# Max pass in pairs of two through four PSUM banks, and two experts' lower products from 16-bit halves, in a one-core block kernel

## What is computed

```python
xn = layernorm(x)
# branch 1: state scan
xf = depthwise_conv3(xn) + conv_b
dt = sigmoid(xf @ dt_w.T + dt_b) * 0.099 + 0.001
s[t] = exp(dt[t] * A) * s[t-1] + dt[t] * xf[t] * b      # 16 states a channel
y[t] = sum(c * s[t])
# branch 2: attention, then all 8 experts, weighed by a gate
h = layernorm(xn) * g + b
q, k, v = h @ Wq, h @ Wk, h @ Wv          # 16 heads of 64
p = softmax(causal(10 * l2norm(q) * q_scale @ (l2norm(k) * k_scale).T))
o = layernorm(concat(p @ v) @ Wo)
gate = softmax(o @ gate_w + gate_b)
hid = gelu(einsum('bsd,edf->bsef', o, w1) + b1)          # 8 experts, 512 wide
moe = sum_e gate_e * (hid_e @ w2_e + b2_e)
out = x + y + layernorm(moe)
```

## Time and profile before

| | |
|---|---|
| Three executions | 1120.18, 1122.25, 1125.5 us |
| The profiled execution | 1120.17 us, of which the traced span is 1118.4 us |
| TensorE busy | 1075.0 us, 96% of the span |
| DVE busy | 959.6 us, 86% |
| ACT busy | 778.9 us, 70% |
| POOL busy | 277.7 us, 25% |
| TensorE's granted clock | 0.986 of full speed over the span |
| Chain that ended last | 89% of it on TensorE |

### The profile page before, as it was taken

How to read it: one execution, slowest core, us unless ns; L and a number is a source line. 1 busy time by engine, 2 the same in 40 slices (tenths; PEclk the granted TensorE clock), 3 DMA queues, 4 the chain that set the end, 5 groups by cost and what they waited for, 6 DMA issues and landing times.

```text
span 1118.4 us, 27576 instructions
## 1 busy us (share of the span) xinstructions
PE 1075.0 (96%) x10435; PEld 912.2 (82%) x10435; DVE 959.6 (86%) x2543; ACT 778.9 (70%) x1772; POOL 277.7 (25%) x328
## 2 busy tenths in 40 slices
PE   4877999999999999999999999999999999999997
PEld 1664888888888888888888888888888888888897
DVE  8988798898988989898898989889898888988763
ACT  5873948668595876859677594867759587685653
POOL 2340314224031231404123140412403132140200
PEclk9995999999999999999999999999999999999999
DMA  7010000000000000000000000000000000000000
GB/s 210 7 39 10 2 11 7 1 16 1 11 7 11 6 2 16 1 11 6 6 11 2 11 7 11 6 1 16 2 11 6 11 7 6 6 6 1 7 2 10
DMA packets 18722, 14.60 MB, mean 13 GB/s; under 512 B 2408, under 2 KB 16160, under 8 KB 18592
## 3 DMA queue, kind: packets, MB, share of 16 engines
q1 hardware_dynamic: 17680, 12.76, 3.8%
q10 hardware_dynamic: 912, 0.09, 0.1%
HBM read 10.75 MB, written 2.10 MB: 11 GB/s over the span
## 4 chain that ended last, share of the span: by engine, by line
PE 89%; DVE 4%; issue 3%; ACT 2%; POOL 1%; SPq 0%; DMA 0%; POOLq 0%; DVEq 0%; ACTq 0%
PE O L565 19%; PE O L468 14%; PE S L484 5%; PE U L547 5%; PE U L548 5%; PE U L549 5%; PE J L382 5%; PE S L449 4%; PE J L343 4%; PE U L449 4%; PE S L404 4%; PE J L344 3%; PE J L345 3%; PE S L400 3%; PE O L475 2%
## 5 line engine op out<-in xcount | busy, mean ns | idle before, releaser
L777 ACT ACTIVATE hid<-U,b1c 128x256 f32<-128x256 f32 x512 | 200.5, 474 | 174.8 <-PE U L549 174.7
L565 PE MATMUL O<-w2s,hid 128*128 128x128 f32 x2048 | 251.1, 276 | 0.0
L565 PEld LDWEIGHTS O<-w2s,hid 128*128 128x128 f32 x2048 | 238.6, 192 | 2.9
L928 POOL TENSOR_SCALAR_AFFINE_SELECT P<-P 128x512 f32<-128x512 f32 x128 | 85.0, 664 | 618.6 <-ACT P L750 618.5
L468 PEld LDWEIGHTS O<-Vx,P 128*128 128x128 f32 x1536 | 188.0, 192 | 30.2 <-issue 14.3
L468 PE MATMUL O<-Vx,P 128*128 128x66 f32 x1536 | 188.6, 273 | 3.6 <-POOL P L928 2.0
L1198 DVE TENSOR_TENSOR_SCAN st<-aexp,u 128x256 f32<-128x256 f32 x256 | 178.8, 698 | 0.4 <-issue 0.3
L920 POOL TENSOR_TENSOR raw<-raw,nr 128x512 f32<-128x512 f32 x124 | 132.8, 1097 | 134.9 <-DVE nr L1066 134.9
L1208 DVE SCALAR_TENSOR_TENSOR y<-st,bc,y 128x256 f32<-128x256 f32 x240 | 133.5, 556 | 8.5
L547 PE MATMUL U<-h2h,w1h 128*128 128x256 f16 x480 | 130.9, 273 | 0.0
L549 PE MATMUL U<-h2h,w1l 128*128 128x256 f16 x480 | 130.9, 273 | 0.0
(11 more groups left out here) (204 smaller groups left out, 2048.0 us busy)
## 6 DMA issues: line engine op xcount, KB each, us to landing
xin<-in_L_attn_x SPq DMA_DIRECT2D x16, 128.0 KB, 2.1
xres<-in_L_attn_x SPq DMA_DIRECT2D x16, 128.0 KB, 2.3
hid<-in_L_ffn_w SPq DMA_DIRECT2D x2, 1024.0 KB, 6.5
out_dram<-fin SPq DMA_DIRECT2D x16, 128.0 KB, 1.8
raw<-in_L_ffn_Wq SPq DMA_DIRECT2D x1, 512.0 KB, 4.7
raw<-in_L_ffn_Wk SPq DMA_DIRECT2D x1, 512.0 KB, 6.4
raw<-in_L_ffn_Wv SPq DMA_DIRECT2D x1, 512.0 KB, 7.4
wos<-in_L_ffn_Wo SPq DMA_DIRECT2D x1, 512.0 KB, 11.4
```

Of the source, the lines that this page charges most:

```text
L565: last = mm(O[e % 2][:, t * P:(t + 1) * P], hid[:, e % 2, m, t * P:(t + 1) * P], w2s[:, e * FC + m, :], start=(m == 0), stop=(m == FC - 1))
L777: fn(hid[:, e % 2, f % FC, :], U[q % 2][:, m * SEQ:(m + 1) * SEQ], ACT.Gelu_apprx_tanh, bias=b1c[:, f:f + 1], scale=1.0 / WS).then_inc(gel ...
```

## The change

The change has two parts, with moves that they need.

1. *Lower products of experts 0 and 1 from 16-bit halves* (`NH = 2`). Once, `w2` of the two experts is split into `w2h` and `w2l` (ACT in body 0, DVE in body 1). For each sequence ACT copies the 128x1024 hidden values to 16 bit (`hidden_high`), DVE takes the rest (`hidden_low`), and `expert_down` runs three 16-bit products where one float32 product stood: 24 instructions an expert for 16. `hidh` and `hidl` are one buffer each, so `hidden_high` of expert 1 waits for the lower product of expert 0. DVE also makes `gate64`, the two experts' gates divided by 64.
2. *Max pass two pairs at a time.* The two `J` banks, now one tile `J2`, serve beside `S2`. The products of two pairs stand one behind the other, then their masks. The pass has four turns, in m = 2, 5, 6 and 7.
3. *Moves.* `step_sizes(i+1)` and `turn(i+2)` go from m = 7 and 6 to m = 1 and into `S2`; `g_step` 6 goes to k = 8 of the attention half and `g_step` 7 to 9 to m = 1; the convolution goes to k = 9; one state leaves the attention half; the first turned maxima use a bank of `U2`. `turn_qk` 4 and 5 wait for the maxima of the first turn.

```diff
-        MAX_AT = {1 + p: (p,) for p in range(NP)}
+        MAX_AT = {2: 0, 5: 2, 6: 4, 7: 6}
...
+                if s > 0 and n in (4, 5):
+                    pe.wait_ge(mx_done, s * 2 * NP + 4)
...
+                elif p == 0:
+                    pe.wait_ge(ex_done, s * NP)
+                    pe.wait_ge(wo_copied, s)
+                    pe.wait_ge(tanh_done, s + 1)
+                    if s < LAST:
+                        pe.wait_ge(g_vec, (s + 1) * KG + 12)
+                    pe.wait_ge(t_lo, s * NL + 4)
+                    max_products(s, p)
+                else:
+                    pe.wait_ge(t_lo, s * NL + NL)
+                    pe.wait_ge(mx_done, s * 2 * NP + 2 * p)
+                    max_products(s, p)
+                max_products(s, p + 1)
+                max_masks(s, p)
+                max_masks(s, p + 1)
...
-                pe.wait_ge(gelu_done, s * NE * FC + FC * (e + 1))
+                if e < NH:
+                    pe.wait_ge(hid_low, s * NH + e + 1)
+                    pe.wait_ge(w2_low, 1)
...
+                        if e < NH:
+                            mm(dst, hidh[:, m, q], w2h[:, f, :], start=(m == 0), stop=False)
+                            mm(dst, hidh[:, m, q], w2l[:, f, :], start=False, stop=False)
+                            last = mm(dst, hidl[:, m, q], w2h[:, f, :], start=False, stop=(m == FC - 1))
...
+            def hidden_high(s, e):
+
+                act.wait_ge(gelu_done, s * NE * FC + FC * (e + 1))
+                from_one(act, w2_ready, s * NE + e if e > 0 else (s - 1) * NE + NH)
+                fn(hidh[:, :, :], hid[:, e % 2, :, :], ACT.Copy).then_inc(hid_high, 1)
...
+            def hidden_low(s, e):
+                dve.wait_ge(hid_high, s * NH + e + 1)
+                V.tensor_tensor(hidl[:, :, :], hid[:, e % 2, :, :], hidh[:, :, :], ALU.subtract).then_inc(hid_low, 1)
...
-            G_AT = {0: (0, 1), 3: (2,)}
+            G_AT = {0: (0, 1), 3: (2,), 8: (6,)}
-            SCAN_AT = {1: (0,), 3: (1,), 5: (2,), 6: (3,), 8: (4,), 9: (5,)}
+            SCAN_AT = {1: (0,), 3: (1,), 5: (2,), 6: (3,), 9: (4,)}
```

More of the change, by code:

```diff
@@ L140, in build @@
         hid = sb("hid", [P, 2, FC, SEQ])
+        hidh = sb("hidh", [P, FC, SEQ], F16)
+        hidl = sb("hidl", [P, FC, SEQ], F16)
+        w2h = sb("w2h", [P, NH * FC, D], F16)
+        w2l = sb("w2l", [P, NH * FC, D], F16)
+        gate64 = sb("gate64", [P, T, NH])
         acc = sb("acc", [P, T, D])
@@ L642, in body @@
                         turn_gate(i - 1, (i + 1) * NP)
-                    if new:
-                        for p in MAX_AT.get(m, ()):
-                            scores_for_max(i + 1, p)
+                    if new and m == 1:
+                        step_sizes(i + 1)
+                    if newer and m == 1:
+                        turn(i + 2)
+                    if new and m in MAX_AT:
+                        scores_for_max(i + 1, MAX_AT[m])
                     if old and 1 <= m < NE:
@@ L876, in body @@
                         copy_output(i)
+                    if old and m == 0:
+                        hidden_high(i - 1, 0)
+                    if not old and m == 5:
+                        act.wait_ge(d_w2, 16)
+                        fn(w2h[:, :, :], w2s[:, 0:NH * FC, :], ACT.Copy, scale=WS).then_inc(w2_high, 1)
                     if not new and m == 6:
@@ L1153, in o_step @@
                                         ).then_inc(o_vec, 1)
+                    for t in range(T):
+                        V.tensor_scalar(gate64[:, t, :], ge[:, t, 0:NH], grs[:, t:t + 1], 1.0 / WS, ALU.mult,
+                                        ALU.mult).then_inc(o_vec, 1)
                 elif n == 14:
@@ L1355, in body @@
                             g_step(i + 2, n)
+                    if new and k == 9:
+                        for n in range(3):
+                            convolve(i + 1, n)
                     if k != 6:
@@ L1375, in body @@
                             norm_step(i + 1, 1, n)
+                    if old and m == 0:
+                        for d in (6, 7):
+                            scan(i, d)
+                            add_state(i, d)
                     if old and 2 <= m <= NE:
@@ L1386, in body @@
                         low(i + 1, TURN_AT[m] + 1)
-                    if new:
-                        for p in MAX_AT.get(m, ()):
-                            maxima(i + 1, p)
+                    if newer and m == 1:
+                        g_step(i + 2, 7)
+                        g_step(i + 2, 8)
                     if old and m == 1:
```

126 lines of the change are left out of this document (68 added, 58 removed).

## The result

The changed kernel took **1180.47 us** (median of four executions, 1179.05 to 1180.95); the kernel before took 1121.28 us beside it. The ratio is **1.0518** (95% interval 1.0489 to 1.0548), so the change is slower by 59 us. The forecast was slower by 36 us, and its range ended at 1178 us.

What follows compares the result with a forecast made beforehand. TensorE was taken to bound the 66.2 us body. Waits of 4.4 less savings of 1.7 gave 2.7 us a body, 35 over 13 bodies, plus 2 elsewhere: 1157, as a median 1158 us; range 1126 to 1178 us.

Steps and rivals of the forecast that it cites:

- five waits of TensorE on DVE: m = 1 to 3: gateT 0.8, first hidl 0.8, hT 0.8, second hidl 1.0, maxima 1.0; 4.4 us a body.
- TensorE's saving: Per body: 0.82 us from two experts' 16-bit lower products and 0.88 from the paired max pass, together 1.7.
- rival 4: Lower products: 99 ns weight loads set the 16-bit pace, 24 take 2.4 us; 1190 us; chance 0.05.
- the 2.05 us ahead of `add_expert`: DVE's room per body before the change: waits for TensorE, read as eight pieces of at most 0.6 us.
- Two states behind `nr`: DVE ahead of gateT: POOL's scalings add 0.60 us to each state, so two states take 3.44 us.
- Rival 3: Behind nr, each of two y and hidl waits a whole POOL scaling, 1.01 us; 1178 us; chance 0.06.
- Rival 2: Behind nr, no meeting with POOL: states take 1.12 us, hidl unhindered; +1.2 a body, 1138 us; chance 0.16.
- flat allowance: Outside bodies 1 to 13: prologue and body 0 unchanged within 3 us; bodies 14, 15 and tail +2 us.

Runs made afterwards that it cites:

- the two runs without halves and fillers: Changed kernel without the 16-bit halves, max pass alone: 1152.86 us; the same with late states and expert_up ahead of the turns: 1120.94 us.
- The run with the max pass and fillers: Changed kernel without the 16-bit halves, plus twelve filler products of 256 columns, written over later, ahead of gated_b2: 1138.33 us.
- the best version: Changed kernel with states 6 and 7 late, expert_up ahead of the turns, and 16-bit halves for the first expert only: 1114.25 us, 0.9919.

## Why the prediction was right in direction and too low in size

**Right.** The bound, and where it would go: five waits of TensorE on DVE, 5.8 us from start to start against 4.4. TensorE's saving: the lower product takes 1.34 us (24 rows 56 ns apart at full clock; 1.38 forecast), so rival 4, weight loads that set the pace, is out. A step of m = 5 to 7 with two pairs takes 4.09 us (4.1 forecast), where one with one pair took 3.70. From `turn_qk` in m = 3 to the next output product a body is 1.38 us shorter than before (51.93 against 53.31); the forecast's steps give 1.36. Normalisations and convolution moved `low` by 0.43 us (0.4 forecast). One slip of reading had no effect: the 2.05 us ahead of `add_expert` lie in four pieces a body, since the eight of the earlier trace rows are those of two bodies.

**The step that failed is "Two states behind `nr`".** It priced each state at 1.12 + 0.60, because in the earlier trace rows only the `y` of such a state was long. There the scan took its usual 0.68 although a pair of scalings was running, and the grouped row of POOL doesn't show where within the pair it fell. A narrower window on the trace before, which could have been read ahead of the forecast, does:

```profile
526.19 1.44 POOL L920 TENSOR_TENSOR raw<-raw,nr 128x512 f32<-128x512 f32 x1
```

That scan started at 526.11, just as one scaling ended and 0.08 us ahead of the next. So it was first; the scaling took 1.44 us instead of about 1.0, and only `y` came behind. In the changed kernel the second scan comes behind a scaling as well, and takes 0.84 us longer. Two states came to 4.29 instead of 3.44 us, and `hidl`, priced at +0.3, met POOL for +0.5. Followed through, that is 0.85 + 0.21 and 0.12 of small hand-overs: `turn_qk` in m = 3 starts 5.24 us later in its cycle than before (576.92 against 544.59 + 27.09), not 4.06. Bodies 1 to 13 cost 49.5 us where 35 were forecast: 14.4 of the 23.5 us by which the growth of the span (60.5) outran the forecast (37).

**Rival 3 was nearer in kind, and its time is in part luck.** It charged a whole scaling to both `y` and to `hidl` and gave 1178 us. Measured, a scan, two `y` and `hidl` lose 0.84 + 0.60 + 0.60 + 0.52 = 2.6 us together, against 1.5 in the forecast and 3.0 in the rival. The Trainium skill ("SBUF — State Buffer", section "Who interferes with whom") lets the later one of the two engines wait until the other's instruction has ended. The trace agrees in kind: the scan that starts ahead of POOL is not held up (0.68), the ones behind are, by the rest of a scaling rather than by all of it (each ends 0.1 to 0.2 us sooner than the scaling's end and its own usual time would make it). I read one row's 0.60 as the price of every state, where by the rule it matters who is first; what is then left of a scaling differs from row to row. The rival's 1178 us lie close to 1180 also because its bodies are too long (1.5 us more than the forecast's, where 1.1 were measured) and it leaves out the same 9 us as the forecast, told below.

**Rival 2** (no meeting, 1138 us) was tried by shortening POOL: 1149.81 us, a body of 68.02 where the rival's +1.2 makes 67.4. A fifth of the meeting (0.5 of 2.6 us) was still there, on the second state.

**The other 9 us** lie where the forecast had set a flat allowance. Prologue and body 0 cost 4.0 us, taken as 0 within 3. In the prologue the first output product comes 1.9 us later, and the clock in the stretch from 28 to 32 us (before, then after) is different:

```profile
28.00:32.00 4.00, 3.02 (x34) 2.02 (x31) 3.52 (x10) 2.68 (x5) 2.81 (x3) 1.00 0.02 7
```

```profile
28.00:32.00 4.00, 3.73 (x25) 3.17 (x26) 2.85 (x6) 1.50 (x4) 3.54 (x4) 0.57 0.02 6
```

In the runs the first output product comes at 71.8 us where that clock stays up (before, and the two runs without halves and fillers) and at 73.0 to 75.3 where it falls. The run with the max pass and fillers has no halves and is hit as well (75.06), so the halves are not needed for it; what decides it was not settled. Bodies 14, 15 and the tail cost 7.1 us, where 2 were forecast. From the output product of body 14 to that of body 15 it is 4.1 us, forecast as 1.1, with three waits that the trace before does not have: `gateT` 2.1, maxima 1.0 and one `hidl` 0.9. From there to the end it is 3.0 us, forecast as 0.8. One row of TensorE's waits from each stretch (who waited for whom: total, times, longest):

```profile
PE O L561 <- DVE gateT L1213: 2.1, 1, 2.1
```

```profile
PE O L603 <- DVE hidl L1233: 4.3, 4, 1.5
```

In the stretch to the end TensorE waits for each of the four `hidl`, 4.3 us where the forecast had charged one wait of 1.2 in body 15 and one in the tail. The halves are the cause of this part: the stretch takes 64.3 us here and with the halves alone, 61.5 in the two runs without halves and fillers, and 61.3 before.

## What to carry to other kernels

Before an operation goes into a gap on DVE, look at what POOL does in that stretch: the gap may be there because DVE was reading PSUM or idle while POOL had the SBUF. A saving on the bounding engine is worth nothing if the second engine has to feed it in a fixed order; add up the chain from the late operand to the next one on both engines, and move what nobody waits for behind it. Here the place of two states and the order of a few steps were worth 56 us (1180.47 against 1124.89), while the best version gains 0.8%, about 9 us, on the kernel before.

## What was not expected of the hardware

- TensorE's granted clock falls to 0.50 behind short waits: 1.58 and 0.83 us in the kernel after, 1.31 us in the run with the max pass alone. In the body shown it was 0.50 from 569 to 573 us and came back to 1.00 by 575 us, while TensorE was busy. Not every body is hit: in the kernel after, the body at 707 us has the same first two waits and kept 1.00, and what decides it was not settled. What such a spell costs depends on who is later: nothing beside a busier DVE, 1.06 us a body where TensorE is the bound, 0.7 to 2.7 us with POOL held back.
- POOL's hold reaches instructions that had been thought safe: a scan (0.68 to 1.52 us), a cast from one SBUF tile to another (0.29 to 1.07) and the first of two normalisations in the attention half (`xn`, 128x128, 1.22 us where the kernel before, which does it elsewhere, takes 0.34).
